# Layer 1's opening: batch 1's last value copies and first query/key copies placed ahead of the weighting and combination of batch 2's expert rows

## The reference

```python
# layer 0, end: the two chosen experts of each token, weighted, times a gate, added to x
moe = jnp.einsum('te,etc->tc', cw, eo).reshape(B, N, C)
x = x + g_mlp[:, None, :] * moe
...
# layer 1, beginning
y = _modulate(_layer_norm(x), m0, m1)
qkv = y @ qkv_w + qkv_b
q, k, v = jnp.split(qkv, 3, axis=-1)
...
attn = jax.nn.softmax(jnp.einsum('bhqd,bhkd->bhqk', q, k) / math.sqrt(hd), axis=-1)
```

## Time and profile before

| | us |
|---|---|
| median of 3 runs | 1536.67 (1532.54 to 1538.28) |
| the profiled execution, its time | 1528.52 |
| the profiled execution, its span | 1526.8 |

### The profile page before, as it was taken

How to read it: one execution, slowest core, us unless ns; L and a number is a source line. 1 busy time by engine, 2 the same in 40 slices (tenths; PEclk the granted TensorE clock), 3 DMA queues, 4 the chain that set the end, 5 groups by cost and what they waited for, 6 DMA issues and landing times.

```text
span 1526.8 us, 26992 instructions
## 1 busy us (share of the span) xinstructions
PE 1413.6 (93%) x8989; PEld 967.9 (63%) x8989; DVE 1219.2 (80%) x2569; ACT 928.5 (61%) x1675; POOL 721.8 (47%) x1620
## 2 busy tenths in 40 slices
PE   7999999989999999896899999899999999989998
PEld 5653334768899887784643334888875333468885
DVE  7779996886987687666899997676977999876664
ACT  4449997455666554563369987444744899754432
POOL 0656560114766433126555666767766666671000
PEclk9999999989999999998899999999998999999999
DMA  7765530128654554325745532211065454100001
GB/s 205 223 182 129 146 92 3 39 88 247 178 156 120 173 132 130 99 82 183 215 136 139 136 72 7 47 7 20 4 184 183 121 147 111 8 4 1 1 1 63
DMA packets 108247, 160.71 MB, mean 105 GB/s; under 512 B 33860, under 2 KB 75830, under 8 KB 107976
## 3 DMA queue, kind: packets, MB, share of 16 engines
q1 hardware_dynamic: 101964, 142.85, 30.7%
q0 software_dynamic: 6144, 16.14, 8.5%
HBM read 114.74 MB, written 39.58 MB: 101 GB/s over the span
## 4 chain that ended last, share of the span: by engine, by line
PE 35%; DVE 33%; issue 4%; ACT 3%; DMA 2%; SPq 2%; another core or an unknown queue 1%; POOL 0%; DVEq 0%; ACTq 0%
PE psum L1658 16%; DVE minus_max L2696 11%; PE psum L2144 6%; PE psum L2287 5%; DVE minus_max L2691 4%; DVE x_norm L2534 2%; PE psum L1811 1%; PE psum L1848 1%; DVE bn L2506 1%; DMA raw_a<-in_L_cond_b 1%; PE psum L1721 1%; DVE hid_lo L3291 1%; PE psum L1992 1%; PE psum L1837 1%
## 5 line engine op out<-in xcount | busy, mean ns | idle before, releaser
L1577 ACT ACTIVATE probs<-psum 128x512 f32<-128x512 f32 x768 | 403.3, 600 | 67.5 <-PE psum L1837 60.5
L2696 DVE TENSOR_REDUCE minus_max<-psum 128x1 fp32r<-128x512 f32 x606 | 376.5, 682 | 33.6 <-PE psum L1811 32.8
L1811 PE MATMUL psum<-k_stack,q_stack 54*128 54x512 f32 x768 | 257.3, 460 | 9.8 <-DVE minus_max L2696 3.9
L1658 PE MATMUL psum<-x_split,w_hi 128*128 128x512 f32 (+1 forms) x684 | 244.8, 401 | 7.4 <-issue 2.4
L1837 PE MATMUL psum<-q_stack,k_stack 55*128 55x512 f32 x768 | 239.6, 445 | 8.3 <-ACT probs L1577 8.2
L1837 PEld LDWEIGHTS psum<-q_stack,k_stack 55*128 55x128 f32 x768 | 116.7, 187 | 162.3 <-ACT probs L1577 153.9
L1096 POOL TENSOR_TENSOR qr_m<-qr_m 64x8 f32<-64x8 f32 (+35 forms) x544 | 197.7, 363 | 42.6
L1848 PE MATMUL psum<-probs,o_t 128*19 128x512 f32 x1536 | 205.0, 606 | 6.1 <-ACT o_t L1556 3.2
L1811 PEld LDWEIGHTS psum<-k_stack,q_stack 54*128 54x128 f32 x768 | 112.6, 187 | 93.1 <-DVE minus_max L2696 71.5
L1091 POOL TENSOR_TENSOR qr_m<-qr_rows 64x288 f32<-64x288 f32 (+31 forms) x64 | 44.7, 698 | 252.1 <-DMA qr_rows<-qr_rows 252.1
L1658 PEld LDWEIGHTS psum<-x_split,w_hi 128*128 128x128 f32 x684 | 129.8, 192 | 31.7 <-issue 7.1
(11 more groups left out here) (452 smaller groups left out, 3185.3 us busy)
## 6 DMA issues: line engine op xcount, KB each, us to landing
qk_parts_d<-qk_parts SPq DMA_DIRECT2D x48, 512.0 KB
raw_b<-in_L_cond_w SPq DMA_DIRECT2D x36, 432.0 KB
q_stack<-qk_parts_d SPq DMA_DIRECT2D x96, 144.0 KB
k_stack<-qk_parts_d SPq DMA_DIRECT2D x96, 144.0 KB
raw_a<-in_L_cond_w SPq DMA_DIRECT2D x36, 384.0 KB
q_stack<-qk_parts_d SPq DMA_DIRECT2D x96, 72.0 KB
k_stack<-qk_parts_d SPq DMA_DIRECT2D x96, 72.0 KB
moe_out_d<-branch SPq DMA_DIRECT2D x9, 576.0 KB, 3.4
```

Of the source, the lines that this page charges most:

```text
L1577: act.activation(PE_[:, v // 4, 2 * hf + pr, :], psum[:, score_bank(16 * i + v), :], ACT.Exp, scale=SCALE).then_inc(s_e, 1)
L1658: i = pe.matmul(dst, a, r, start=(n == 0), stop=(n == len(terms) - 1))
L1811: return pe.matmul(psum[:, bank, :], Q6[half(hf, STK), g, pr, P * qt:P * qt + P], K6[half(hf, STK), g, pr, :], start=True, stop=True)
L2696: dve.tensor_reduce(MX[:, i % 2, col:col + 1], psum[:, bank, :], AX.X, ALU.max, negate=True).then_inc(s_mx, 1)
```

## The change

On ACT, the copies of value tiles 2 and 3 of batch 1 and of query/key chunk 0 come ahead of the first weighting of batch 2. Chunk 1 comes ahead of the second weighting, chunk 2 behind the third, and chunk 3 behind the fourth. On DVE, the rest of chunk 0 comes ahead of the first combination of batch 2, the rest of chunk 1 ahead of tiles 1 and 2, the rest of chunk 2 ahead of tile 3, and the rest of chunk 3 ahead of `normalise(1, 0, 2)`. Nothing is added or removed, and PE, POOL and SP have the same order as before.

```diff
--- before.py
+++ after.py
@@ -1506,15 +1506,14 @@
                 turned(1, 0, 1, (1,))
                 values(1, 0, (1,))
                 turned(1, 0, 1, (2,))
+                values(1, 0, (2, 3))
+                qk_hi(1, 1, (0,))
                 weigh(2, (0,))
-                values(1, 0, (2,))
-                weigh(2, (1,))
-                values(1, 0, (3,))
-                qk_hi(1, 1, (0,))
-                weigh(2, (2,))
                 qk_hi(1, 1, (1,))
+                weigh(2, (1, 2))
+                qk_hi(1, 1, (2,))
                 weigh(2, (3,))
-                qk_hi(1, 1, (2, 3))
+                qk_hi(1, 1, (3,))
                 weigh(3, (0,))
                 qk_hi(1, 1, (4,))
                 weigh(3, (1,))
@@ -2637,15 +2636,16 @@
                 split_lo(("p", 1), RAWP, WPH, WPL, WPT)
                 qk_rest(1, 0, (4,))
                 low(1, 0, 1)
-                combine_rows(2, (0, 1))
                 qk_rest(1, 1, (0,))
-                combine_rows(2, (2,))
+                combine_rows(2, (0,))
                 qk_rest(1, 1, (1,))
+                combine_rows(2, (1, 2))
+                qk_rest(1, 1, (2,))
                 combine_rows(2, (3,))
                 rsqrt(2)
-                qk_rest(1, 1, (2,))
+                qk_rest(1, 1, (3,))
                 normalise(1, 0, 2)
-                qk_rest(1, 1, (3, 4))
+                qk_rest(1, 1, (4,))
                 combine_rows(3, (0, 1))
                 low(1, 0, 2)
                 combine_rows(3, (2, 3))
```

## The result

| | us |
|---|---|
| kernel before, median of 14 runs | 1531.53 (1521.21 to 1538.28) |
| changed kernel, median of 14 runs | 1534.55 (1527.84 to 1538.94) |
| ratio, 95% interval | 1.0040 (1.0021 to 1.0058), that is +6.1 us (+3.2 to +8.9) |
| changed kernel, the profiled execution, its time and span | 1535.58, 1533.9 |

The changed kernel is slower by 0.4%, inside the half per cent that counts as the same. The medians as such differ by 3.0 us; the ratio pairs runs taken near each other, and goes by 6.1. The forecast of 1540.7 started from a median of three runs of the kernel before, 1536.67; the fourteen runs have 1531.53.

A forecast was written before the change was run, and what follows sets the result against it. From 713 us on DVE was taken to set the time, so two combinations of 2.0 us moved out of its wait are paid, all else nothing: 1536.67 + 4.0 = 1540.7 us, range 1531 to 1547.5.

The forecast's parts named there:

- The copies waited for PE's signals, not for the weightings: ACT, value tiles 2 and 3: copies start when PE's late signals arrive, 703.28 and 712.46 as before, whatever the weightings' order.
- first rival: ACT's weightings did hold the copies; chunk 0's rest starts 8.66 us earlier, combinations add 4.0: -4.6 us, 1532.1; chance 0.20.
- ACT's part is worth nothing: Moving two value copies and one chunk copy ahead of weightings gains nothing; the first weighting's delay is just covered.
- the 0.2 us of slack: First weighting on ACT ends by 713.80, and DVE needs it at 714.01: delay covered with 0.2 us to spare.
- Two combinations come out of the hole and are paid: DVE's combinations of tiles 0 and 1 move behind the wait for chunk 0: +4.0 us, upper bound 6.0.
- the 8 to 9 forecast: PE's wait for `x_norm` of batch 2 before its turn, 4.00 us before, was to become 8 to 9.
- 14.1 forecast: Sign in the changed profile: `x_norm` of batch 2 stands 14.1 us behind the rest of chunk 0, 9.5 before.
- The rest of chunk 3, costed at nothing: DVE, ahead of `x_norm` of batch 2: delays the turn 0.6 us, given back at the low part; cost nothing.
- second rival: Combinations beside POOL's arithmetic 6.0 us, `x_norm` of batch 3 and others about 1, lower PE clock 1.5: +8.5, 1545.2; chance 0.13.
- The second rival's clock term: PE, idle 8 us instead of 4.00, starts batch 2 at the lower clock; one chunk there costs 1.5 us more.

The follow-up runs named there:

- first pair: The first profiled executions, one of the kernel before (1528.52 us) and one of the changed kernel (1535.58 us), taken ahead of the experiments.
- among the experiments: Kernel before and changed kernel, both unaltered, run again in the experiments' series: changed 1518.22 us against 1510.11, ratio 1.0043.
- DVE's half alone: DVE's order as in the changed kernel, ACT's order as in the kernel before; against the kernel before 1515.95 us, ratio 1.0048.
- the filled one: Kernel before with all four batch 2 weightings ahead of value copies 2 and 3, all four combinations and normalising ahead of chunk 0's rest: 1516.55 us, ratio 1.0050.
- kernel before with the stall by hand: Kernel before plus 36 small chained copies on ACT ahead of the copy of value tile 3; 1518.29 us against 1511.20, ratio 1.0053.

## Why the prediction was right

**The copies waited for PE's signals, not for the weightings.** The second half is shown. The first pair has 10.92 us of idle time in front of three copies with no weighting between them, and the other traces show it from the other side: without the stall the same weightings stand between the same copies, and neither value copy waits. The first half is argued. The value copies wait for no other semaphore than their products', but the profile names no instruction as releaser ("remote"), the ends of products are modelled, and ACT is the engine that waits in all three stalls. A signal that comes late and an ACT that takes it late would look the same here. The first rival (1532.1) needed the copy of tile 3 at about 700.5; it came at 711.83. How the hole was split among the copies was off: the forecast had tile 3's at the very end, and the last to be let through was chunk 0's; tile 3's came 18.63 us behind the first gather instead of 22.87, and no run shows why. What matters, the restart of DVE behind the first gather, stayed: 23.82 and 23.51.

**ACT's part is worth nothing.** Right only in company. In the changed kernel the delayed weighting is covered by DVE's own wait for chunk 0. Alone it cost 5.6 us. "Worth nothing" rested on the other half having already spent the same time; the 0.2 us of slack that I named was to DVE's new order.

**Two combinations come out of the hole and are paid: 4.0 us, at most 6.0.** The mechanism is right: moving DVE's steps alone costs all of it, and without the two combinations the time of before is back. In the first pair `x_norm` went from 33.31 to 37.83 behind the first gather, +4.5, and the first Exp by +3.8; the wait on PE is 8.27, inside the 8 to 9 forecast, and `x_norm` stands 14.32 us behind the rest of chunk 0 (14.1 forecast). By the runs the time rose by 6.1 us (3.2 to 8.9), 6.5 among the experiments, and 7.3 (4.1 to 10.6) with DVE's half alone. So 4.0 is inside the first two intervals, just under the third and below all three figures; the upper end of the forecast was nearer. The 14.1 was hit in part by luck: two more combinations at 1.91 and 1.92 us and the rest of chunk 3 make 4.4 of the 4.83 us, the first combination took 2.56 instead of 2.99, and `rsqrt` and the statistics 3.42 instead of 2.61. Among the experiments DVE's hole was 2.6 us and not 12, and the two combinations moved `x_norm` by no more than that; that the time rose by as much all the same comes from what stands behind, and was not taken apart further.

**The rest of chunk 3, costed at nothing.** It was to delay the turn by 0.6 us and be given back at the low part. The 0.6 us is seen in front of `x_norm` in every trace of the new order. That it was given back isn't: in the first pair both the turn and the first Exp come 3.8 us later, and among the experiments the turn comes 4.5 and the Exp 5.4 us later.

**The term that was mis-sized is what stands beside POOL.** I took 4.0 because the combinations would meet POOL's arithmetic no more than before, left `x_norm` of batch 3 to the second rival, at about 1 us, and didn't cost that of batch 2. It matters, and the sign isn't fixed: 1.44 us where POOL stands idle, 2.58 beside POOL (the changed kernel among the experiments). In the first pair it went the other way, 2.14 before and 1.44 after, which took 0.7 us off on the way from +4.5 to +3.8. Among the experiments `x_norm` started only 3.2 us later, and the first Exp came 5.4 later. The Trainium skill, in "SBUF — State Buffer", "SBUF: two separate sides", has one lock for the port pair that VectorE and GpSimd share; a VectorE instruction takes it with two SBUF inputs or in a mode that uses both ports. `x_norm` has one tile as input, and whether it ran in such a mode no run shows. Its length agrees with waiting: the 1.14 us lie under POOL's two steps of 0.67 and 0.69 together. What the rule doesn't foresee is that POOL's steps on a single column cost `x_norm` nothing, up to 0.58 us long (1.44 us beside four of them, kernel before with the stall by hand).

**PE's clock.** The second rival's clock term isn't seen. The granted clock of 0.86 in 733 to 752 us, against 0.99 before, comes from the windows: the turn of batch 2 stands at 732.92 in the changed kernel and at 725.50 before. In the 19 us from the turn on the clock is 0.86 in the changed kernel and 0.85 before, and among the experiments 0.91 and 0.92, although PE had been idle for 8.27 instead of 4.00 us and for 8.30 instead of 3.28. In the first pair PE's first value step behind the turn takes 0.60 us in both orders, and 0.30 some 3 us later, so PE starts there at the lower of the two levels with either order.

**The time of the whole.** In the profiled pair the spans differ by 7.1 us. 3.6 of it had arisen before the first gather, where nothing is changed, and 3.8 by the first Exp. Of one pair of executions only the second part may be read as the change's. The measured median of 1534.55 lies inside the range of 1531 to 1547.5, but so would the first rival's 1532.1 have done (its own sum, 4.0 less 8.66 us, gives 1532.0), and it is nearer to it than to the forecast's 1540.7. The place in the range therefore decides nothing: 5.1 of the 6.2 us under the forecast is the median of before, which three runs had put too high. What decides are the difference of +6.1 us, the waits in front of the copies, and the experiments.

## What to carry to other kernels

Before moving a step to in front of a wait, ask what the engine was doing during that wait: work that lies in the hole is free, and a reorder that "unblocks" the waiting step pays for it, in full where the wait is long. Here the idle time in front of a step belonged to that step's own releaser, so look at when its input was ready, and not at what stands between it and the one before. Two engines' orders that fit each other should be costed together and apart, since either half can cost the whole; and an order tuned to a long hole (the filled one) lost 7.6 us where the hole was missing. And windows at the same clock time in two traces don't show the same work: line them up on an instruction ahead of the change first.

## What the hardware showed

- The same kernel took 1531.5 us in the first series and 1510 to 1511 in all later ones. Three places where ACT went on late behind PE's finished products cover the difference: 8.28 us idle at 524.87, 3.41 at 669.60, and 11.16 at the change; in the first trace of the changed kernel the same three are 9.13, 3.49 and 10.92. All three lie in bursts of indirect gathers on POOL, whose pace was the same (mostly 1.25 us each) where ACT waited and where it didn't. So the gathers by themselves don't do it. What does stays open: nothing here could be switched to bring it about, the number of the first series' chip isn't known, and I can't tell another chip from another condition of one. Two chips (0 and 8) don't show it.
- The Trainium skill says in "SBUF — State Buffer", "SBUF: two separate sides", that PE and ACT never wait on another engine's port. The later traces agree, with 0.32 us idle at 518.45 instead of 8.28 and neither value copy waiting; whether a port is what ACT waited for in the first two no run shows.
- DVE's `x_norm`, with one tile as input, takes 1.44 us for its four instructions with POOL idle or at steps on one column, and 2.14 to 2.58 beside POOL's steps on 268 and 269 columns (batch 2's, first trace of before and changed kernel among the experiments; 1.89 where fewer of them fell beside it).
